# The order of five engines and the PSUM banks from a planner that models durations, in place of delays behind TensorE's steps

## The reference, cut to what matters

```python
xn = _layernorm(x, axis=-1)
x = x + _L0_attn_ref(xn, ...) + _L0_ffn_ref(xn, ...)
# attention: 32 query heads and 8 key/value heads of 128, 4-bit weights with one scale for each 128 rows
w = (qw.astype(jnp.float32) - 8) * jnp.repeat(scales, 128, axis=0)
q, k, v = xn @ wq, xn @ wk, xn @ wv          # q and k are then rotated (cos, sin)
scores = q @ k.T / sqrt(128)                 # causal mask, softmax over keys
out = (softmax(scores) @ v) @ wo
# the other layer: xn @ W_base.T + b_base + 2 * ((xn @ A) * combine) @ B, combine from a top-2 router
```

## Time and profile before

| | us |
|---|---|
| median of 3 runs | 2034.65 (2032.78 to 2037.78) |
| profiled execution, its own time | 2025.33 |
| its span, first to last instruction | 2023.5 |
| TensorE busy in the span | 1832.8 (91%) |
| VectorE, ScalarE, GpSimd busy | 1542.1 (76%), 1305.1 (64%), 1153.6 (57%) |

### The profile page before, as it was taken

One profiled execution on the slowest core, in us unless ns is written; L12 is line 12 of the kernel. 1 busy time (PEld: TensorE's weight loads), 2 busy tenths in 40 slices (PEclk: granted clock), 3 DMA queues, 4 the chain that ended last, 5 costly groups with the idle time before them and its releaser, 6 DMA issues.

```text
span 2023.5 us, 29277 instructions
## 1 busy us (share of the span) xinstructions
PE 1832.8 (91%) x9580; PEld 1494.8 (74%) x9580; DVE 1542.1 (76%) x3082; ACT 1305.1 (64%) x2775; POOL 1153.6 (57%) x1085
## 2 busy tenths in 40 slices
PE   9898999999999999999878699898999999999997
PEld 6786777877787777877657577786777777777775
DVE  6757887788878787688756577877887788868885
ACT  3136777677767777577645466665776677766764
POOL 1135666566666666466563355655667566666653
PEclk8999999999999999999989899998999999999999
DMA  6305445244543455344723634534354444435443
GB/s 214 105 1 141 115 131 139 86 131 110 136 125 105 101 140 136 89 125 114 215 73 113 179 100 126 136 89 115 105 132 107 126 115 131 127 92 131 114 145 111
DMA packets 284623, 244.18 MB, mean 121 GB/s; under 512 B 32660, under 2 KB 213944, under 8 KB 284472
## 3 DMA queue, kind: packets, MB, share of 16 engines
q1 hardware_dynamic: 281160, 236.54, 43.3%
q0 software_dynamic: 2112, 4.19, 0.7%
q10 hardware_dynamic: 1200, 1.59, 0.2%
HBM read 164.40 MB, written 77.86 MB: 120 GB/s over the span
## 4 chain that ended last, share of the span: by engine, by line
PE 50%; DVE 21%; ACT 8%; issue 7%; POOL 6%; DMA 6%; SPq 1%; DVEq 0%; POOLq 0%
PE ring L1664 16%; PE O_ps L1509 13%; PE ring L1509 7%; DVE rope L1344 7%; PE ring L1599 6%; PE ring L1600 5%; ACT ring L1092 3%; DVE rope L1339 3%; DMA moved<-squares 3%; PE ring L1675 3%; DVE Y L1407 3%; DVE PT_low L1236 2%; ACT probs L1077 2%; DVE probs L1360 2%; POOL rope L928 2%
## 5 line engine op out<-in xcount | busy, mean ns | idle before, releaser
L1092 ACT ACTIVATE ring<-ring,ratios 128x512 f32<-128x512 f32 x736 | 472.8, 668 | 147.3 <-PE ring L1600 144.5
L1077 ACT ACTIVATE probs<-probs,negmax 128x128 f32<-128x128 f32 (+7 forms) x512 | 394.0, 771 | 198.7 <-DVE negmax L1360 197.1
L1360 DVE CUSTOM_DVE_ANT_0 probs<-ring,mask_row 128x128 f32<-128x128 f32 (+7 forms) x512 | 376.3, 753 | 101.5 <-PE ring L1664 100.3
L921 POOL TENSOR_TENSOR moved_low<-moved,moved_high 128x512 fp32r<-128x512 f32 x256 | 325.1, 1289 | 155.6 <-ACT moved_high L1000 154.5
L928 POOL TENSOR_TENSOR rope<-rope 128x512 f32<-128x512 f32 x160 | 206.0, 1287 | 328.0 <-DVE rope L1344 327.5
L1236 DVE TENSOR_TENSOR PT_low<-ring,PT_high 128x512 fp32r<-128x512 f32 (+3 forms) x515 | 249.3, 488 | 167.2 <-ACT PT_high L1000 132.5
L1000 ACT ACTIVATE PT_high<-ring 128x512 fp32r<-128x512 f32 (+3 forms) x515 | 223.9, 441 | 171.2 <-PE ring L1675 159.1
L1664 PE MATMUL ring<-K_high,Q_high 128*128 128x512 f32 (+3 forms) x768 | 242.2, 370 | 55.7 <-DVE PT_low L1236 23.1
L1599 PE MATMUL ring<-xnT_high,W 128*128 128x512 f32 x640 | 280.0, 438 | 11.9 <-ACT ring L1092 9.8
L957 POOL TENSOR_TENSOR ctx_low<-ctx_f,ctx_high 128x512 fp32r<-128x512 f32 x128 | 165.4, 1292 | 192.7 <-ACT ctx_high L1000 191.0
L1675 PE MATMUL ring<-ident,probs 128*128 128x128 f32 x1280 | 225.9, 280 | 36.2 <-DVE PT_low L1236 29.0
(11 more groups left out here) (149 smaller groups left out, 3746.3 us busy)
## 6 DMA issues: line engine op xcount, KB each, us to landing
squares<-probs SPq DMA_DIRECT2D x256, 256.0 KB, 2.0
moved<-squares SPq DMA_DIRECT2D x256, 256.0 KB, 5.8
R_sb<-row_sums SPq DMA_DIRECT2D x128, 256.0 KB, 3.5
raw<-in_qw_q SPq DMA_DIRECT2D x64, 256.0 KB, 4.1
raw<-in_qw_o SPq DMA_DIRECT2D x64, 256.0 KB, 3.5
raw<-in_qw_k SPq DMA_DIRECT2D x16, 256.0 KB, 2.9
raw<-in_qw_v SPq DMA_DIRECT2D x16, 256.0 KB, 3.1
stage<-in_scales_v SPq DMA_DIRECT2D x16, 256.0 KB, 4.1
```

Of the source, the lines that this page charges most:

```text
L921: nc.gpsimd.tensor_tensor(out=low, in0=moved[:, :, j, :], in1=high.bitcast(f32), op=ALU.subtract).then_inc(moved_done, 1)
L1077: nc.scalar.activation(probs[:, at], probs[:, at], ACT.Exp, bias=negmax[:, i:i + 1], scale=-1.0, accum_out=sums[:, i:i + 1]).then_inc(exp_ ...
L1092: nc.scalar.activation(place(step), place(step), ACT.Copy, scale=ratio(step)).then_inc(rescaled, 1)
L1360: nc.vector.tensor_tensor_reduce(row, ps, hidden_keys, -1.0, -MASKED, ALU.add, ALU.min, negmax[:, i:i + 1]).then_inc(negmax_ready, 1)
```

## The change

No instruction's kind, shape or number changes in the main computation; the order of the instructions and the banks do. The patterns are written anew, one for each of a unit's four heads in place of shared ones. `AFTER`, `WEIGHT_SPAN`, `length`, `begins`, `behind`, `weights_due` and `ring_places` go. A new function `plan` runs through the program once at build time as a list scheduler. It has a queue for each kind of work on each of five engines, a duration for each kind (`seconds`, `TAKES`, `STRETCHES`), a latency for each DMA (`LANDS`), a time for a semaphore to wake each engine (`WAKES`), and for each piece of work what it awaits. At each turn the engine that can begin first takes, among its kinds, the one that can begin within 0.03 us of the first and is wanted soonest; SP takes what is ready first. What "wanted" means is the time of the TensorE step that needs it, less a number from `SLACK`. TensorE may take a step of a kind out of the written order where the model says that the next one would wait, up to 9 us ahead (`AHEAD`). A bank is chosen by when the model sees VectorE empty it, and projections, outputs and value rows leave one bank spare (`SPARE`).

```diff
-WEIGHT_SPAN = 96.0
-FIRST = "F T O O F T F O T V O F V F V F T F O F O O O V"
-EARLY = "F T F O O T F T F V T F V O F F O F O O V O O F F V"
-LATE = "T S S S T S T V S S T V V V V S S V V V"
+FIRST = "F O T O F T F O F T V V F V F T F O F O O O V"
+SECOND = "F T F O O T F T F V F T V O F F O F O O O V O F V F"
+FIRST_LATE = "T S S T S S T V S S T V V V V S S V V V"
...
-AFTER = {
-    "SP sums": 5.7,
...
-    "DVE rope": 0.7,
...
-def ring_places(steps):
...
+def seconds(step):
+
+    kind = step[0]
+    if kind == "scores":
+        return 3 * sum(max(0.109, 0.4435e-3 * n) for n in (min(step[3] + 1, MOVED) * P, (step[3] + 1 - MOVED) * P) if n > 0)
...
+TAKES = {"low": 0.62, "square": 0.63, "inverse": 0.12, "norm": 0.99, "add": 0.67, "linear": 0.67, "row": 0.61, "terms": 2.3,
...
+LANDS = {"sums_out": 2.6, "sums_in": 3.6, "out": 1.9, "in": 7.5, "load": 4.0, "x_row": 3.4, "store": 4.4, "parked_y": 8.0, "last_rows": 8.0,
...
+WAKES = {"PE": 0.235, "ACT": 0.18, "DVE": 0.15, "POOL": 0.12, "SP": 0.07}
+AHEAD, SPARE, CROWDED = 9.0, 1, 6.0
+SLACK = {"high": 2.7, "low": 1.2, "max": 3.8, "exp": 2.8, "far": 15.7, "inverse": 9.0, "norm": 1.2, "rescale": 1.5, "terms": 7.6,
...
+def plan(steps):
...
+    def awaited(op):
...
+        if kind == "low":
+            step = tuple(at)
+            if step[0] == "turn":
+                n = turn_at[step]
+                return [("high", *step)] + ([("values", *turns[n - LOWS][1:])] if n >= LOWS else [])
...
+    def wanted(op):
...
+        if kind in ("high", "low"):
+            step = tuple(at)
+            return at_us[("values", *step[1:]) if step[0] == "turn" else step] - SLACK[kind]
...
+        if kind in ("terms", "sum", "split"):
+            u, w, c = at
+            return at_us["scores", u, 0 if w == "k" else int(w[1]), 4 * c] - SLACK[kind]
...
+    def room(step):
+        n = 2 if step[0] == "scores" and step[3] >= 4 else 1
+        free = [bank_free(m) for m in range(BANKS)]
+        late = sorted(free)[n + SPARE - 1] if SPARE and step[0] in ("project", "output", "rows_v") else 0.0
+        now = clock["PE"]
+        best = min(range(BANKS - n + 1), key=lambda lo: (max(now, *free[lo:lo + n]), max(now, free[lo - 1]) if lo else 1e9, max(free[lo:lo + n])))
+        return max(max(free[best:best + n]), late), best, n
+
+    def best_of(e):
...
+            if e == "PE" and at_us[op] > far and (chain(op) not in places or op[0] == "values"):
+                continue
+            t = ready(e, op)
...
+            found.append((max(t, clock[e]), at_us[op] if e == "PE" else t if e == "SP" else wanted(op), c, op))
+        if not found:
+            return None
+        first = min(x[0] for x in found) + 0.03
+        return min((x for x in found if x[0] <= first), key=lambda x: x[1])
...
-    STEPS = tensor_order()
-    PLACES = ring_places(STEPS)
+    ORDER, PLACES, _ = plan(tensor_order())
+    STEPS = ORDER["PE"]
...
-            for n in range(len(STEPS) + 1):
-                for _, u, h, i in sums[n]:
+            for kind, *of in ORDER["SP"]:
+                if kind == "sums_out":
+                    store_sums(*of)
...
-                for _, u, w, c, k in projected[n]:
-                    if k + 1 == KT:
-                        terms(u, w, c)
+                elif kind == "terms":
+                    terms(*of)
```

More of the change, by code:

```diff
@@ new lines, with chain, emptied @@
+STRETCHES = {"max": (0.075, 0.1335), "exp": (0.285, 0.107)}
+WAKES = {"PE": 0.235, "ACT": 0.18, "DVE": 0.15, "POOL": 0.12, "SP": 0.07}
+STALLED = 0.09
+def chain(step):
+    return step[:4] if step[0] in ("project", "output") else ("base", *step[1:]) if step[0] == "lora_b" else step
+def emptied(step):
+    kind = step[0]
+    if kind in TURNED:
+        return ("low", *step)
+    return {"scores": ("max", *step[1:]), "rows_v": ("value_low", *step[1:]), "project": ("terms", *step[1:4]),
+            "output": ("add", *step[1:4]), "lora_a": ("lora_read", *step[1:]), "base": ("linear", *step[1:]),
+            "finish": ("row", *step[1:])}[kind]
@@ new lines, in earlier @@
+def earlier(u, h, n):
+    return divmod(head_index(u, h) - n, REP)
+TURNED = ("turn", "turn_x", "turn_hidden", "turn_scales")
+EMPTIES = ("low", "max", "value_low", "terms", "add", "linear", "row", "lora_read")
+AHEAD, SPARE, CROWDED = 9.0, 1, 6.0
+SLACK = {"high": 2.7, "low": 1.2, "max": 3.8, "exp": 2.8, "far": 15.7, "inverse": 9.0, "norm": 1.2, "rescale": 1.5, "terms": 7.6,
+         "sum": 4.4, "split": 2.7, "read": -5.0, "value": -4.2, "context": -0.9, "context_low": 5.8, "moved": 1.2,
+         "moved_low": 3.5, "weight": 6.3}
@@ L1112, in _ @@
             root(PARKED, 0, 2)
[L1113 to L1117 removed]
+            for kind, *of in ORDER["ACT"]:
+                if kind == "rescale":
+                    rescale(tuple(of))
+                elif kind == "high":
+                    s = tuple(of)
                     high(*s)
@@ L1431, in _ @@
             row_stats(PARKED, 3)
-            turned_now, scored = behind(STEPS, AFTER["DVE turn"], *TURNED), behind(STEPS, AFTER["DVE max"], "scores")
-            summed, finished = behind(STEPS, AFTER["DVE sums"], "scores"), behind(STEPS, AFTER["DVE norm"], "values")
-            others = behind(STEPS, AFTER["DVE add"], "output", "lora_a", "lora_b", "finish")
-            projected = behind(STEPS, AFTER["DVE rope"], "project")
-            value_rows_made, squares_due = behind(STEPS, AFTER["DVE rows"], "rows_v"), behind(STEPS, AFTER["DVE squares"], "scores")
-            for n in range(len(STEPS) + 1):
-                for s in turned_now[n]:
+            for kind, *of in ORDER["DVE"]:
+                if kind == "low":
+                    s = tuple(of)
                     low(*s)
```

634 lines of the change are left out of this document (400 added, 234 removed).

## The result

| | before | with the change |
|---|---|---|
| median, us | 2033.72 (2024.43 to 2037.78, 4 runs) | 1871.39 (1862.75 to 1876.18, 4 runs) |
| ratio | 1 | 0.9203 (95%: 0.9156 to 0.925) |
| profiled execution, span, us | 2023.5 | 1868.6 |
| granted clock over the span | 0.972 | 0.983 |

What follows compares the result with a forecast made beforehand. TensorE was taken as the bound, leaving its 190 us idle and its clock to gain: 58 - 18 + 26.8 + 8.7 + 3 = 78.5 us, so 2034.65 - 78.5 = 1956 us, forecast 1925 to 1990, range 1903 to 2028.

Steps and rivals of the forecast that it cites:

- The middle: 190 us around the change of sequence: 26.8 of 31.5 us of extra idle go, plus 8.7 us of clock.
- The long stretches: Whole units, 230 to 1010 and 1200 to 1980 us: 58 of 111.2 us idle go, 18 return, net 40.
- the slower rival: Moved tiles land late and stop ScalarE, holding VectorE and TensorE: 1.4 us a head, 90 us, 2046 us; chance 0.11.
- value steps and rescales: First long stretch: half of 12.7 us (value steps) and 7.9 us (rescales) goes, 6.4 and 4.0 us.
- turns and scores for a bank: First long stretch: two thirds of 26.3 us of waits until VectorE has made `PT_low` go, 17.5 us.
- New waits: Long stretches: early steps meet full banks or late operands, 0.49 us in 37 of 64 heads, 18 us back.
- PE's busy time falls by some 9 us: Sign of being right: TensorE's work stays the same; the clock's return in the middle gives 8.7 us.
- The sum's own floor: Whole kernel: all waits but a tenth gone and the clock back whole gives 1864 us; needs everything right.
- No engine is short of time here; the order is wrong by one place: Long stretches: VectorE does `terms` before `PT_low`, so TensorE stands 1.88 us in the example; terms' scores are a head away.
- VectorE's order and the banks: Long stretch: `PT_low` ahead of `terms` and banks chosen by modelled emptying save 17.5 of 26.3 us.
- More comes back: Rival: clock outside the middle (21.7 us) and the middle's other 8.7 return, new waits near 0; 1908 us; chance 0.15.
- The rule on short idles of the Trainium skill: Long stretches: small idles between matmul groups make the clock swing; by it all the clock lacks there would return.

Runs made afterwards that it cites:

- experiment 2: The kernel before, with TensorE not waiting for rescales and ScalarE doing a same-sized instruction on a row of its own instead; ratio 0.9994.
- kernel 12: The changed kernel with loads planned to land after 5.5 us and TensorE allowed chains due up to 20 us later; ratio 0.9101, median 1843.53 us.
- Experiment 1: The kernel before, with VectorE's rotation terms placed 2.6 us behind the projection, not 0.7; ratio 1.0823.
- Experiment 3: The kernel before, with planned orders for VectorE, ScalarE, GpSimd and SP, TensorE's order and the banks kept; ratio 1.0224.
- kernels 10: The changed kernel with packed weight loads planned to land 5.5 us after issue, not 4.0; ratio 0.9129.

## Why the prediction was right in sign and half in size

**Right: what would change.** Turns waiting for `PT_low` were to fall below 6 us and fell to none, scores likewise and fell to 3.6; the store of finished rows was to follow VectorE within 3 us and follows at 2.4 (1063.71 to 1066.09). The middle was to lose 26.8 us of idle time and lost 31.5. Start and end gave 3.7 us for 3. The long stretches are idle for 26.3 and 26.4 us per 780, where 34 were expected. ScalarE's waits for moved tiles to land fell from 44.1 us in 35 cases to 18.7 in 17 over the span, 0.3 us a head where over 1 was the sign, so the slower rival fell. The middle has one wait just over the 5 us that was the mark, 5.15, for a moved tile.

**Wrong, first: the long stretches.** The sum had 58 us gone and 18 put back, 40 net; idle time fell by 62.9 us (111.2 to 48.3). The terms that were too small, in both long stretches together: of the waits for value steps and rescales the sum took half, "because the stretch of scores and values has little other work in it", and 34.1 of 41.3 us went (26.2 to 6.1, 15.1 to 1.1). Of the waits of turns and scores for a bank it took two thirds, and 45.4 of 52.2 us went. New waits did come, 22.9 us where 18 were put down, but not the scattered short ones that the sum named: `moved_low` went from 5.7 us to 18.8 (7.5 + 11.3), `ctx_f` is 5.5 us in a single wait, and turns wait 4.3 us for `probs`. So some 86 us were taken away and 23 given back.

**Wrong, second, and larger: only TensorE's idle time was counted, "PE's busy time falls by some 9 us".** It fell by 56.9. The clock explains some: the busy time of each window by what its clock lacks of 1 gives 52.5 us before and 31.2 after, so 21.3 us where 8.7 were forecast, with window clocks rounded to hundredths (half a hundredth of 1800 us is 9). The rest, 35.6 us, is read here as the part of the waits that lies at the weight loads under matmuls still recorded. It is what is left over and not measured by itself; experiment 2 is the run that shows such a part, some 26 us when 62.4 us of short waits at the weight loads were taken away. The sum opened with "the work on TensorE stays the same, so the change can only touch two things: the 190 us in which TensorE stands still, and the clock". That sentence is the failed step: there were 306.5 us of waits and not 190. The sum's own floor shows it too. It put 1864 us for all waits but a tenth gone and the clock back whole, "which needs everything to go right" and would leave some 59 us of idle time (190.7 - 100 - 31.5); the change came within 8 us of that with 92.7 us of idle time left, and kernel 12 went below it, 1843.53 us, with 74.6 left (1841.4 - 1766.8). The forecast's 78.5 falls short of the span's 154.9 by 28 us of idle time (98.0 - 69.8), 12.6 us of clock (21.3 - 8.7) and these 35.6.

The table shows that the waits at the weight loads are the better measure. The rival is to count idle time at the matmuls: then what is left of the span is the matmuls' busy time, and over the eleven kernels at a clock of 0.97 or more it differs by 73.5 us (1766.8 to 1840.3). What is left without the waits at the weight loads is their own time (1491 us in the change) and gaps that no wait accounts for, and it hardly moves: between 1705 and 1727 us in the same eleven kernels, while their spans differ by 182 us. The three kernels above that, at 1740 to 1767, are those with the clock at 0.964 or less.

**Wrong, third: "No engine is short of time here; the order is wrong by one place".** The sum held late terms to be free since their "scores are a head away". Experiment 1 shows that they hold a bank all that time: put later with the banks as they were, they cost 8.2%. Experiment 3 shows that planned orders in the old banks lose 2.2%, which a sum that priced "VectorE's order and the banks" in one line could not tell. And more than half of the gain (0.9775 to 0.9295, 4.8 of 8 points) comes from TensorE's freedom to take later steps, which the sum gave 10.4 of its 27.9 us. It covers most of the rescales: 62.4 us at the weight loads became 8.6.

**The rivals.** "More comes back" came nearest (1908), with a larger return of the clock, which was right, and new waits near 0, which was not; it counted no hidden part either. The rule on short idles of the Trainium skill, weighed in the prediction ("TensorE: Matmul & The Clock Gate", section "A second HAM failure mode: psum-queue depth-cycling"), would have had the long stretches come back to 1. In the change they stand at 0.99 and 0.99 (0.99 and 0.98 before), though most short waits are gone; the middle, where the long waits were, went from 0.88 to 0.95. There the row served better than the rule. In kernels 10 and 12, with still fewer waits, both long stretches read 1.00, so what the last hundredth hangs on is not settled by the change alone.

## What to carry to other kernels

Count TensorE's waits at its weight loads, not as the matmuls' idle time, before saying what there is to win; here the one was 306.5 us, the other 190.7. That is not a forecast of what one removed group gives: 62.4 us of it, taken away alone, gave nothing. Where every engine issues in a fixed order, expect little from removing one group of short waits, or from moving one kind of work: here the waits moved to another line. Ask of each piece of work which bank it holds until it is done. Orders, banks and the freedom to go ahead pay together, and then the planner's durations are worth correcting from the trace: with one DMA latency at 5.5 us and not 4.0 the ratio went from 0.9203 to 0.9129. Judge such a correction on the chip. The planner's own reckoning ends at 1768 us for the change and at 1794 for that kernel, and ranks them the wrong way round.

## What the runs showed of the hardware that was not expected

The granted clock over a span went with the waits: 0.948 and 0.949 in the two slowest kernels, with 445.4 and 312.1 us at the weight loads, 0.992 and 0.993 in those with 132.6 and 135.0. It isn't the total alone, for the kernel before had 306.5 us and 0.972.

What a long wait costs besides its length can be seen once in the rows. After the wait of 5.15 us shown above, which ended at 932.43, the granted clock from 932 to 938 us is 0.63, which is mostly the lower level. The three matmuls of 512 columns that follow the wait start 0.60, 0.42 and 0.43 us before the next one. From 938 on the clock is 1.00 again, and the same three start 0.22 to 0.24 us before the next:

```profile
939.48 0.39 PE L1737 MATMUL O_ps<-moved_high,V_high 128*128 128x512 f32 x1
939.70 0.39 PE L1737 MATMUL O_ps<-moved_low,V_high 128*128 128x512 f32 x1
939.93 0.40 PE L1737 MATMUL O_ps<-moved_high,V_low 128*128 128x512 f32 x1
```

TensorE was busy for 5.57 of these 6 us; at 0.63 that is work for 3.5 us at the full clock, so this one wait cost some 2 us on top of its 5, an estimate. The DMA engines carried 355 GB/s in the same 6 us, against some 130 in the long stretches; whether that had a part in it is not separated.
